# A two-layer decoder on one core: two chunks of a projection moved ahead of a block boundary, a buffer fill moved from GpSimd to VectorE, and sixteen additions moved behind a small conversion

## What is computed

```python
# layer 0, feed-forward: 16 experts (one per row) and a shared expert
shared = jax.nn.silu(x @ w_gate.T) * (x @ w_up.T) @ w_down.T
out = shared + expert_out.sum(axis=0)
...
# layer 1, cross-attention, 16 heads over a context of 1601 rows
scores = jnp.einsum('bhqd,bhkd->bhqk', qh, kh) * scale
attn = jax.nn.softmax(scores, axis=-1)
out = jnp.einsum('bhqk,bhkd->bhqd', attn, vh)
return concat @ Wo + bo
```

## Time and profile before

| | |
|---|---|
| median of 3 runs | 1512.67 us (1511.65 to 1512.72) |
| the profiled execution | 1512.28 us, of which the span of its instructions 1510.5 us |
| busy share of the span | TensorE 91%, VectorE 70%, ScalarE 51%, GpSimd 22% |
| mean granted TensorE clock | 0.948 of full speed |
| experts' block | ends about 547 us |
| combine block | about 554 to 660 us |
| last heads loop | about 864 to 1420 us |

### The profile page before, as it was taken

The page is one execution under the profiler, slowest core; times in us unless marked ns, Lnnn a source line. Parts: engine busy times, 40 slices in busy tenths (PEclk is TensorE's granted clock), DMA queues, the critical chain, the costliest instruction groups (busy, mean ns, idle before and its releaser), DMA issues. The chain is left out here.

```text
span 1510.5 us, 24918 instructions
## 1 busy us (share of the span) xinstructions
PE 1374.6 (91%) x9358; PEld 763.6 (51%) x9358; DVE 1060.9 (70%) x2349; ACT 774.5 (51%) x1066; POOL 325.4 (22%) x409
## 2 busy tenths in 40 slices
PE   6898899989999979748998888999999999999996
PEld 3565488847898966413334522333333333333285
DVE  4886566661212228667994887999999999997077
ACT  2344366621111102315764315788887888888754
POOL 4110322252000027643334550000000000000011
PEclk9999899999999989858999968999999999999999
DMA  9548533366898822774430650233322234320001
GB/s 341 186 149 244 157 131 122 125 214 214 272 301 283 295 96 60 200 204 127 135 93 21 189 185 1 67 76 98 89 66 66 66 92 97 75 66 2 1 1 56
DMA packets 153353, 198.69 MB, mean 132 GB/s; under 512 B 16235, under 2 KB 125311, under 8 KB 153106
## 3 DMA queue, kind: packets, MB, share of 16 engines
q1 hardware_dynamic: 141516, 165.34, 36.5%
q0 software_dynamic: 9200, 29.64, 6.4%
q10 hardware_dynamic: 2518, 2.13, 0.4%
HBM read 136.08 MB, written 60.70 MB: 130 GB/s over the span
## 5 line engine op out<-in xcount | busy, mean ns | idle before, releaser
L2127 DVE TENSOR_REDUCE xa_part<-psum 128x1 f32<-128x512 f32 (+1 forms) x768 | 462.5, 661 | 24.8 <-PE psum L1980 22.7
L2079 ACT ACTIVATE xa_P<-psum 128x1024 f32<-128x1024 f32 (+1 forms) x416 | 403.2, 1020 | 103.5 <-PE psum L2004 102.9
L2004 PE MATMUL psum<-sa_Q,xa_K 48*128 48x512 bf16 (+3 forms) x1664 | 266.7, 380 | 4.0 <-DMA sa_Q<-xa_mrow 2.9
L1980 PE MATMUL psum<-xa_K,sa_Q 48*128 48x512 bf16 (+1 forms) x768 | 239.0, 388 | 4.5 <-DVE xa_part L2127 1.5
L2020 PE MATMUL psum<-xa_P,xa_V 128*32 128x512 f32 (+1 forms) x1664 | 222.6, 607 | 0.4 <-ACT xa_P L2079 0.4
L1980 PEld LDWEIGHTS psum<-xa_K,sa_Q 48*128 48x128 bf16 x768 | 59.2, 94 | 232.5 <-DVE xa_part L2127 160.7
L2004 PEld LDWEIGHTS psum<-sa_Q,xa_K 48*128 48x128 bf16 (+3 forms) x1664 | 105.3, 97 | 69.0 <-ACT xa_P L2079 21.2
L2124 DVE CUSTOM_DVE_ANT_0 psum<-psum,cf_sb 128x512 f32<-128x512 f32 (+3 forms) x256 | 119.5, 522 | 25.7 <-PE psum L1980 24.7
L1328 PEld LDWEIGHTS psum<-xtT,wgu 128*128 128x128 f32 x992 | 115.5, 192 | 5.8 <-issue 4.6
L1328 PE MATMUL psum<-xtT,wgu 128*128 128x128 f32 x992 | 115.9, 275 | 1.4 <-issue 0.8
L2079 ACT ACTIVATE sa_P<-psum 128x1024 f32<-128x1024 f32 (+3 forms) x128 | 83.4, 702 | 44.0 <-PE psum L2004 43.9
(11 more groups left out here) (243 smaller groups left out, 2141.7 us busy)
## 6 DMA issues: line engine op xcount, KB each, us to landing
wgu<-in_f_gu SPq DMA_DIRECT2D x31, 1024.0 KB
xa_K<-kx SPq DMA_DIRECT2D x192, 100.1 KB, 5.1
wdn<-in_f_dn SPq DMA_DIRECT2D x31, 512.0 KB
vx<-xv_v SPq DMA_DIRECT2D x48, 256.0 KB, 3.4
xa_V<-vx POOLq DMA_DIRECT2D x16, 768.0 KB, 6.4
sa_Q<-qs SPq DMA_DIRECT2D x64, 96.0 KB, 2.3
sa_K<-ks SPq DMA_DIRECT2D x64, 96.0 KB, 2.3
sa_Q<-qx SPq DMA_DIRECT2D x64, 96.0 KB, 2.3
```

What stands on the lines that cost most here:

```text
L1980: last = pe.matmul(out[:, 0:width], hb.q(u)[tile:tile + HALF, to, qt * P:(qt + 1) * P], hb.k(u)[tile:tile + HALF, to, cut[e]:cut[e] + widt ...
L2004: last = pe.matmul(out(j), hb.k(u)[tile:tile + depth, to, kt * P:kt * P + r], hb.q(u)[tile:tile + depth, to, q0(kt):L], start=(half == 0), ...
L2079: act.activation(Pr[0:r, (u * KT + kt) % PR, h:h + 2, 0:w_], S_PS(p)[0:r, :, 0:w_], ACT.Exp, scale=SCALE).then_inc(s_exp, 1)
L2127: dve.tensor_reduce(part[:, g % 2, col + qt, e:e + 1], src[:, 0:cut[e + 1] - cut[e]], AX, ALU.max).then_inc(s_1free, 1)
```

## The change

Three edits, in the diff and in the engines' lists:

1. At the end of the experts' block TensorE waits for the shared expert's last item and projects its first two chunks (`DONE = 2`), 16 matmuls into banks 0 and 1. In the combine block it starts with chunk 2, and the semaphore of the projections starts at 2.
2. The fill of `sv_v` is done by VectorE before its first chunk, no longer by GpSimd at step 2.
3. In the last heads loop GpSimd does `parts(0)` before the 16 additions.

```diff
--- before.py
+++ after.py
@@ -60,6 +60,7 @@
 base = lambda h: ROW_TILE * (h % 2)
 place = lambda h, half: half * (G // 2) + h // 2
 ETILES = (N - E) // P + E
+DONE = 2
 
 
 CHUNKS = T // 2
@@ -492,11 +493,11 @@
             self.sent_before.append(self.sent[n % 2])
             self.sent[n % 2] += 16 * len(kts)
 
-    def pool_init(self, pool):
+    def init(self, engine):
         v = self.v[:, :, :, :].rearrange("p u k n -> p (u k n)")
-        pool.memset(v, 0.0).then_inc(self.s_zero, 1)
-        pool.wait_ge(self.s_zero, 1)
-        pool.memset(v.rearrange("p (h w) -> p h w", w=VW)[:, :, HD:HD + 1], 1.0).then_inc(self.s_ones, 1)
+        engine.memset(v, 0.0).then_inc(self.s_zero, 1)
+        engine.wait_ge(self.s_zero, 1)
+        engine.memset(v.rearrange("p (h w) -> p h w", w=VW)[:, :, HD:HD + 1], 1.0).then_inc(self.s_ones, 1)
 
     def act_copy(self, act, n, ps):
 
@@ -780,7 +781,7 @@
             def _(pool):
                 pool.memset(zt[:, :], 0.0).then_inc(s_zt, 1)
                 pool.memset(env.mhalf, -0.5)
-                val.pool_init(pool)
+                val.init(pool)
                 pool.wait_ge(s_zt, 1)
                 pool.wait_ge(s_x, 16)
                 for i in range(0, ETILES, ZR):
@@ -1359,6 +1360,11 @@
                         if j in after_tile:
                             shared_pe(pe, after_tile[j])
                     down(LAST, LAST % R)
+                    pe.wait_ge(s_sh, len(items))
+                    for t in range(2 * DONE):
+                        for k in range(FC):
+                            pe.matmul(PS[:, t * D:(t + 1) * D], hT[:, k, t * P:(t + 1) * P], w["f_wd"][:, k, :],
+                                      start=(k == 0), stop=(k == FC - 1))
 
                 @block.scalar
                 def _(act):
@@ -1556,8 +1562,6 @@
                         tail.pool_rstd(pool, c)
                     if c + AHEAD < CHUNKS:
                         gather(c + AHEAD)
-                    if c == LAG - 2:
-                        val.pool_init(pool)
                     for n in blocks_at(c):
                         sp_.pool_whole(pool, n)
                     for n in blocks_at(c - 1):
@@ -1566,8 +1570,9 @@
 
             @block.tensor
             def _(pe):
+                pe.sem_inc(tail.s_proj, DONE)
                 for c in range(STEPS):
-                    if c < CHUNKS:
+                    if DONE <= c < CHUNKS:
                         tail.pe_proj(pe, c, lambda k: w["f_wd"][:, k, :],
                                      lambda i, k: hT[:, k, (2 * c + i) * P:(2 * c + i + 1) * P])
                     if 2 <= c < CHUNKS + 2:
@@ -1607,6 +1612,7 @@
 
             @block.vector
             def _(dve):
+                val.init(dve)
                 for c in range(STEPS):
                     if c < CHUNKS:
                         u = c % tail.ring
@@ -1932,11 +1938,12 @@
                     pool.tensor_tensor(mh[:, :, 1, :], by(g), mh[:, :, 0, :], ALU.subtract).then_inc(s_mh, 1)
 
                 if not causal:
+                    parts(0)
                     for t in range(T):
                         last = pool.tensor_tensor(env.x[:, t, :], env.x[:, t, :], env.w["x_bo"], ALU.add)
                     last.then_inc(s_xb, 1)
                     pool.wait_ge(s_xb, 1)
-                    for g in range(GROUPS):
+                    for g in range(1, GROUPS):
                         if 2 <= g <= GROUPS - R + 1:
                             reload_v(g - 2, (g - 2) % R)
                         parts(g)
```

## The result

The changed kernel took 1502.3 us (median of 4 runs, 1500.31 to 1504.15); the kernel before, measured beside it, 1512.28 us (4 runs). The forecast was 1509.1 us and its range ended at 1505.5, so it was wrong, by far too small a gain. The profiled execution of the changed kernel took 1504.15 us (span 1502.3), the longest of its four. Shares hardly moved: TensorE 91% (9358 records in both), VectorE 71%, ScalarE 52%, GpSimd 21%, granted clock 0.952 against 0.948.

A forecast was written before the change was run, and what follows sets the result against it. TensorE, busy 91% of the span, was taken as the bound. Edit 3's -4.2 us and +0.6 us for edits 1 and 2 together made -3.6 us, from the median 1512.67 to 1509.1 us; range 1505.5 to 1511.9.

The forecast's parts named there:

- The boundary: Between experts and combine: the barrier's last arrival moves from 549.16 to 553.65, everything behind it 4.49 us later.
- My first rival: At the experts' end: true last arrival near 553, so 7.24 us of matmuls cost nothing; 1504.6 us, chance 0.16.
- the restart: TensorE's start in the combine block: 554.12 before, forecast 558.61.
- the fill: VectorE's memset of 4096 + 128 columns before chunk 0 in the combine: 4.74 us, lower bound 3.52.
- chunk 2's projection: In the combine, TensorE's first projection after the restart: cold clock, 6.4 us, ending at 570.47, 3.11 us later than before.
- the two transposes: In the combine, from the end of chunk 2's projection to the transpose formerly held up: 8.0 us, reaching 578.47.
- Edit 3: Start of the last heads loop: conversion before additions lets the shift run at 903.9 instead of 908.11, gaining 4.2 us.
- The stall: In the combine, GpSimd's memset holds VectorE's small L205 and the transpose at 577.89; removing it gives back 2.53 us.
- Chunks 0 and 1 were no longer waited for: Combine's start: VectorE no longer waits until 560.52 and 563.97 for TensorE's first two projections.
- The projections are hidden: At the experts' end: the added matmuls cost nothing under a later last arrival; -8.1 us, 1504.6 us, chance 0.16.
- VectorE's memset stops the gathers: Combine's start: VectorE's fill locks out GpSimd, first gather written 4.1 us late; total 1511.4 us, chance 0.13.
- The clock stays low: TensorE's clock rise put off by the earlier restart; a second 20 us at half clock gives 1518.3 us, chance 0.06.

The follow-up runs named there:

- e5: Changed kernel with chunk 1's eight matmuls done a second time at the experts' end; 1506.12 us, ratio 0.995 to the kernel before.
- e8: Kernel before with only the experts' stores of `yg` issued and awaited by ScalarE instead of GpSimd; 1509.77 us, ratio 0.997.
- e7: Changed kernel with the experts' stores issued and awaited by ScalarE and one chunk projected ahead instead of two; 1498.86 us, ratio 0.99 to the kernel before.
- e9: Kernel before with edits 1 and 2, the additions left where they were; 1505.85 us, ratio 0.9953.
- e10: The changed kernel run once more, unaltered; 1502.28 us, ratio 0.9925 to the kernel before.
- e2: Kernel before with edit 2 alone, VectorE filling the values' buffers ahead of its first chunk; 1509.06 us, ratio 0.9977.
- e4: All three edits together, the changed kernel run again beside its parts; 1501.92 us, ratio 0.9937 to the kernel before.
- e6: Changed kernel with the wait for the experts' stores moved from GpSimd to SyncE and one chunk projected ahead; 1501.45 us, ratio 0.9919 to the kernel before.
- e1: Kernel before with edit 1 alone, two chunks projected at the experts' end; 1509.12 us, ratio 0.998.

## Why the prediction was wrong

**The boundary, the step that failed.** "I take the whole 4.49, because the landing is the latest event that the rows show." It was the latest that I had read. GpSimd's drain of 3.9 us had its row in the trace before, and with it GpSimd arrives some 4 us after the landing (553.2 against 549.16), and in the changed kernel TensorE's 7.07 us end together with it (552.75 and 552.6). My first rival guessed the size ("if the true last arrival was near 553, the 7.24 us of matmuls cost nothing") and got 0.16. The sentence against it, that barriers and clearing are real work, was not measured: from the drain's end to TensorE's restart at 554.12, with both barriers and the clearing, the trace has 0.9 us, not 4.96, and to the first gather 1.6. e5 to e8 show it by moving the drain's end and TensorE's end separately.

**The size.** The forecast had the transpose of chunk 2 at 34.03 us from the down projections, it came at 28.18: 5.85 us less. By its own terms:

- the restart was put at 558.61, 14.17 us from the down projections' start; VectorE's fill began at 10.67. That is 3.50: the boundary itself is 4.4 us better (gather 10.43 against 14.8), less 0.9 since I started VectorE with TensorE's first instruction, and in fact the fill begins 0.24 us behind the first gather.
- the fill, 4.74 us in the forecast, took 558.17 - 554.51 = 3.66: 1.08. I scaled from a two-input operation; the lower bound, GpSimd's 3.52 us, was the near one. The Trainium skill ("VectorE: DVE Perf Modes", Zero memsets can be issued as uint32) gives a memset one cycle per element, from which I had an estimate of 4.27 us; the row has 3.47, and the measurement decides.
- chunk 2's projection, 6.4 us in the forecast and 5.29 to the transpose behind it: 1.11, since the clock rose 3.0 us after the restart and not 5.4. VectorE ends its norm at the same moment (563.40 + 0.73 = 564.13), so a faster projection would have gained no more, as e7 shows.
- the two transposes, 7.84 us apart and not 8.0: 0.16.

**What was right.** Edit 3: 4.2 us forecast, 4.23 in the profile, 4.24 in e9 against e10 by the idle time before the shift; in run times it was 3.6 us. The stall: the small instruction falls from 3.28 to 0.17 us (0.33 at most elsewhere in that trace, where I had said 0.2), and e2 gives its 2.53 us back as 2.55. Chunks 0 and 1 were no longer waited for.

**The rivals.** "The projections are hidden" is what happened, and its time, 1504.6 us, was still 2.3 us too high. The fill's and the projection's true lengths are 1.4 us of that (5.27 against 3.9 in the stretch), the kernel before's lower median beside this run 0.4. Its reason, "the store's completion may be seen later than it lands", was not the one: GpSimd's wait is over at 549.2. "VectorE's memset stops the gathers" fell: during the fill the gathers start at 554.27, 555.61 and 556.89, 1.3 us apart as ever. VectorE's memset takes no lock against GpSimd. The Trainium skill ("SBUF — State Buffer", Who interferes with whom) has it so for a VectorE instruction with at most one SBUF input outside the two-port modes; the trace agrees, with 3.47 us of VectorE's memset and no gather longer than 1.03 us. "The clock stays low" did not turn the result, but the clock did take part: it is why edit 1 alone gave 1.7 us in its stretch and e8 lost 1.7 us of its gain, and in e4 the rise in pass 2 was put off by 5 us.

**The total.** The two stretches gain 5.27 + 4.23 = 9.5 us; measured were 10.0, 10.2 and 11.3 us in three comparisons. The rest, 0.5 to 1.8 us, has no single place: it is of the size by which the combine's remainder, the block between the loops and the last block scatter from profile to profile. Whether the change has a part in that stays open.

## What to carry to other kernels

At a boundary where all engines meet, list every engine's arrival from the rows of the block's own line, drains included, before you price work put ahead of it; the last landing of a DMA need not be the last arrival. Work of an engine that arrives early is free up to the latest arrival and costs one for one beyond it. Then look at the latest arrival itself: here it was cheaper to let ScalarE issue the block's stores, where the drain behind the wait took 14 ns, than to fill the time that GpSimd's drain left.

## What the runs showed of the hardware

- A drain's row can start while the engine's last operation still runs, so its length alone misleads; what counts is how long it goes on behind the last operation or wait. For GpSimd that was 3.9 us behind the wait for its last store's landing, 4.0 us behind the last store's own instruction (e6), and 2.1 us behind the last scatter (e7). In the kernel before it was 0.5 to 1.5 us at four block ends at which compute came last and DMAs had been issued earlier in the block, and at most 0.1 us at three ends of blocks in which GpSimd issued no DMA. What it does in that time no run tells.
- VectorE's float32 memset ran at 3.47 us for 4096 columns, 0.85 ns each, about as fast as GpSimd's (3.52).
- After the boundary TensorE's first projection behind an idle time of 6.18 us took 5.21 us at a clock of 0.50, then 0.99; behind 1.78 us (e1) or 1.43 us (e7) it took 3.72 us.
